# A separate opening for batch 0, and the first ternary convolution as row pairs with four products per pair

## What is computed

```python
x1  = x + deform(gn(x), w_off, b_off, w_conv)     # 3x3, offsets and masks from a 3x3 convolution with 27 outputs
q1, q2 = ternary(w1), ternary(w2)                 # -1, 0, 1 by thirds of the range of w - mean(w)
y   = gn(x1)
h1  = conv3x3(y, q1)
o1  = relu(batchnorm(h1, gamma1, beta1))          # statistics over all 4 images
o2  = batchnorm(conv3x3(o1, q2), gamma2, beta2)
out = x1 + relu(o1 + o2)
```

## Time and profile before

| | us |
|---|---|
| median of 3 executions (lowest, highest) | 3021.32 (3019.83, 3022.24) |
| the profiled execution's own time | 3026.24 |
| its span, first to last instruction | 3024.2 |
| PE busy (matmul) | 2610.6, 86% |
| DVE busy | 2101.8, 70% |
| ACT busy | 1182.2, 39% |
| POOL busy | 1354.2, 45% |
| DMA moved | 827.35 MB, 274 GB/s over the span |
| mean granted TensorE clock | 0.941 of full speed |

### The profile page before, as it was taken

How to read it: one execution, slowest core, us unless ns; L and a number is a source line. 1 busy time by engine, 2 the same in 40 slices (tenths; PEclk the granted TensorE clock), 3 DMA queues, 4 the chain that set the end, 5 groups by cost and what they waited for, 6 DMA issues and landing times. The chain is left out here.

```text
span 3024.2 us, 37569 instructions
## 1 busy us (share of the span) xinstructions
PE 2610.6 (86%) x11674; PEld 1741.7 (58%) x11674; DVE 2101.8 (70%) x4522; ACT 1182.2 (39%) x2039; POOL 1354.2 (45%) x1262
## 2 busy tenths in 40 slices
PE   3668888888999999999999998989999896999940
PEld 2444444444565555556566665555555676999940
DVE  5577778777777778777777776776766434565665
ACT  1234444444444444444444434344443112232345
POOL 1036655664554555545555555555653002333300
PEclk9879999999999999999999999999999998999975
DMA  4679999999898999989899998999997212111169
GB/s 152 176 258 347 368 355 359 344 364 318 318 339 314 338 347 349 326 307 329 315 329 334 336 315 307 329 335 324 334 329 257 94 53 67 53 56 50 51 257 408
DMA packets 277870, 827.35 MB, mean 274 GB/s; under 512 B 25436, under 2 KB 59228, under 8 KB 276964
## 3 DMA queue, kind: packets, MB, share of 16 engines
q0 software_dynamic: 165888, 604.05, 55.0%
q1 hardware_dynamic: 111844, 221.72, 21.2%
HBM read 740.19 MB, written 85.48 MB: 273 GB/s over the span
## 5 line engine op out<-in xcount | busy, mean ns | idle before, releaser
L360 POOL DMA_INDIRECT G<-pixel_pairs,quad_c x1152 | 1190.2, 1033 | 933.2 <-PE psT L785 639.0
L648 DVE SCALAR_TENSOR_TENSOR G<-G,wts_c 128x256 f32<-128x256 f32 (+1 forms) x2304 | 1259.6, 615 | 171.7 <-DMA G<-pixel_pairs,quad_c 166.9
L748 PE MATMUL psD<-ST,wconv 128*128 128x512 f32 x2304 | 1066.8, 609 | 0.0
L748 PEld LDWEIGHTS psD<-ST,wconv 128*128 128x128 f32 x2304 | 433.3, 197 | 451.0 <-issue 451.0
L410 ACT ACTIVATE G<-G,wts_c 128x256 f32<-128x256 f32 x1152 | 489.6, 497 | 419.4 <-DVE G L648 418.7
L737 PE MATMUL psF<-pf,qw 128*128 128x512 f32 x2304 | 629.4, 422 | 14.6 <-DVE pf L570 7.6
L737 PEld LDWEIGHTS psF<-pf,qw 128*128 128x128 f32 x2304 | 428.5, 189 | 163.0 <-issue 54.2
L445 ACT ACTIVATE ST<-psT 128x1024 f32<-128x1024 f32 x288 | 294.5, 1023 | 481.3 <-PE psT L785 481.1
L785 PE MATMUL psT<-idn,G 128*128 128x128 f32 x2304 | 323.8, 287 | 168.1 <-ACT G L410 167.6
L785 PEld LDWEIGHTS psT<-idn,G 128*128 128x128 f32 x2304 | 277.4, 147 | 247.0 <-issue 122.4
L737 PE MATMUL psA<-po,woff 128*64 128x512 f32 x1152 | 346.9, 449 | 6.3 <-DVE po L570 6.3
(11 more groups left out here) (144 smaller groups left out, 1604.1 us busy)
## 6 DMA issues: line engine op xcount, KB each, us to landing
pixel_pairs<-yT SPq DMA_DIRECT2D x112, 256.0 KB
G<-pixel_pairs,quad_c POOLq DMA_INDIRECT x1152, 6.4
xz<-in_x SPq DMA_DIRECT2D x32, 512.0 KB, 7.1
xres<-in_x SPq DMA_DIRECT2D x32, 512.0 KB, 7.0
x<-x1c SPq DMA_DIRECT2D x32, 512.0 KB, 4.9
h<-h1c SPq DMA_DIRECT2D x32, 512.0 KB, 3.8
out<-h SPq DMA_DIRECT2D x16, 1024.0 KB, 17.5
xo<-in_x SPq DMA_DIRECT2D x24, 640.0 KB, 7.0
```

The source lines that it names most:

```text
L360: pool.indirect_dma_start(out=G[:, i % RING, :], out_offset=None, in_=tbl[d.b].rearrange("y x q c -> (y x) (q c)"), in_offset=bass.Indirec ...
L648: dve.scalar_tensor_tensor(g[:, 0:w], g[:, w:2 * w], wts_c[:, d.p, q * NG + i:q * NG + i + 1], g[:, 0:w], ALU.mult, ALU.add).then_inc(d_ma ...
L748: ins = pe.matmul(psD[:, oc, :], wconv[:, t, k, oc * 128:(oc + 1) * 128], ST[:, k % 3, t, :], start=(k == 0 and t == 0), stop=(k == TAPS - ...
```

## The change

It has two parts.

**The opening.** Stages -2 and -1 are gone; `schedule` starts at s = 0 behind a `head()` of its own on each engine. All of x of batch 0 is loaded at once into slots 0 to 7 of the ring `G` (`x_all`), the raw w1 into the rest of the ring and `x1c`. DVE takes all statistics, ACT normalises in place, PE turns 8 x 8 blocks into `psT`, ACT evacuates into a ring of four buffers, and SP writes the whole table of batch 0. Only the first two chunks of batch 0's offset convolution are done there; chunks 2 to 7 (letter **j**) move into the first six chunks of stage 0, beside the offset convolution of batch 1. Batch 1's statistics (z) lie in the head, interleaved on DVE with the ternary form of w1; its loads are issued by SP between the table writes, each behind a wait on the statistics taken before. The statistics buffer is single from batch 2 on, and so is `xres`.

**The first ternary convolution** takes the form of the second: `planes` on DVE (four operations of 128x512), `planes_hi` on ACT, `planes_lo` on DVE, then four units of 24 matmuls of 256 columns (`f_unit`: output tile, bank), placed at taps 5, 6, 8 and 0 of the next chunk. A unit's products lie in halves of one bank; ACT copies the first (`h1_begin`), DVE adds the others (`h1_rows`: two operations of 128x256, one of 128x512, one batch-norm statistic, for each output tile). The planes `V` and the split planes `pl` are single, except in stage 4, where a second `pl_b` and `psD` are used. ACT takes over the high part of the offset convolution's split (`split_hi`). The middle weights of w1 are made in `winograd_w1`, those of w2 are copied on ACT at the end of stage 4.

```diff
-                for s in range(-2, NB + 1):
+                for s in range(0, NB + 1):
...
+                        just = (ahead(r, rh, p, 2), ahead(r, rh, p, 3)) if s == 0 else (None, None)
+                        f, before = now[3], None
+                        if f and first and s > 1:
+                            before = Chunk(s - 2, NR - 1, NR // 2 - 1, 1, False, True)
+                        elif f and not first and s < NB:
+                            before = f.before()
+                        emit(s, *now, *then, *just, before)
...
+            F_UNITS = {0: [(1, 1)], 5: [(0, 0)], 6: [(0, 1)], 8: [(1, 0)]}
+            F_UNITS_FIRST = {0: [(1, 1)], 6: [(0, 0), (0, 1)], 8: [(1, 0)]}
...
+                for r in range(NR):
+                    sp.dma_start(x_all[:, :, r * PX:(r + 1) * PX], rows_of(x, 0, r * RC, RC)).then_inc(h_load[r], 16)
...
-                    hold(sp, f_split, f.n - 1 + CREDIT)
+                    hold(sp, f_v, f.n - 1 + CREDIT)
...
+                    load_z(Chunk(1, 0, 0, 0, True, False))
+                    load_z(Chunk(1, 1, 0, 1, False, False))
...
+                    for r in range(NR):
+                        sp.wait_ge(h_yt, 2 * (r + 1))
+                        write_table(0, r, yt_ring[r % 4], h_tw[r % 4])
+                        if r == 1:
+                            sp.wait_ge(s_edge, 16 * 4 * NB)
+                            load_j(Chunk(0, 2, 1, 0, False, False))
+                        if 1 <= r < NR - 1:
+                            load_z(Chunk(1, r + 1, (r + 1) // 2, (r + 1) % 2, False, r + 1 == NR - 1))
...
                         load_z(z)
+                    if d:
+                        hold(sp, d_x1, d.n + CREDIT)
+                        sp.dma_start(xres, rows_of(x, d.b, d.r * RC, RC)).then_inc(d_xl[d.p], 16)
...
+                        write_table(o.b, o.r, yT, o_tw)
+                    for c in (fp, f if s == NB else None):
+                        if c:
+                            hold(sp, f_h, CT * (c.n + 1) + CREDIT)
+                            sp.dma_start(rows_of(h1_d, c.b, c.r * RC, RC), h1c[:]).then_inc(f_store, 16)
...
+                            pool.wait_ge(j_split, 2)
+                        else:
+                            hold(pool, o_tw, TW * (d.n + NR) + CREDIT)
+                    hold(pool, o_idx if s else j_idx, d.n + 1)
...
-                        if s == 0 and d.first and i == STAGE1:
+                        if s == 0 and d.first and i == W1_SLOT:
...
+                        y_rows(r)
+                    for r in range(NR):
+                        turned(r)
+                        if r + 3 < NR:
+                            y_rows(r + 3)
+                        if r == 4:
+                            jt_om_evac(Chunk(0, 0, 0, 0, True, False))
+                        if r == 5:
+                            jt_om_turned(Chunk(0, 0, 0, 0, True, False))
...
+                def planes_hi(s, f):
+
+                    act.wait_ge(f_v, f.n + 1 + CREDIT)
+                    act.wait_ge(f_conv, 4 * (f.n if s < NB or f.first else f.n - 1) + FC)
+                    for t in range(CT):
+                        i = act.activation(planes_of(s, f)[:, 0, t, :, 1:W + 1], V[:, t].rearrange("p j i w -> p (j i) w"), ACT.Copy)
+                    i.then_inc(f_hi, 1)
...
+                def planes(f):
+
+                    dve.wait_ge(f_y, f.n + 1)
+                    need(dve, f_hi, f.n)
+                    need(dve, f_split, f.n)
...
+                    for j, (a, b, op) in enumerate(((0, 2, ALU.subtract), (1, 2, ALU.add), (2, 1, ALU.subtract), (3, 1, ALU.subtract))):
+                        i = dve.tensor_tensor(V[:, :, j], xf[:, f.p, :, a:a + 7:2, :], xf[:, f.p, :, b:b + 7:2, :], op)
+                    i.then_inc(f_v, 1)
+
+                def planes_lo(s, f):
+
+                    dve.wait_ge(f_hi, f.n + 1)
+                    dve.wait_ge(f_v, f.n + 1 + CREDIT)
+                    p = planes_of(s, f)
+                    for t in range(CT):
+                        i = dve.tensor_tensor(p[:, 1, t, :, 1:W + 1], V[:, t].rearrange("p j i w -> p (j i) w"),
+                                              p[:, 0, t, :, 1:W + 1].bitcast(F32), ALU.subtract)
+                    i.then_inc(f_split, 1)
...
+                    dve.wait_ge(f_begin, CT * f.n + oc + 1)
+                    dve.wait_ge(f_conv, 4 * f.n + 2 * oc + 2 + FC)
...
+                    dve.tensor_tensor(odd, even, m2, ALU.subtract)
+                    dve.tensor_tensor(even, even, m2, ALU.add).then_inc(f_part, 1)
+                    dve.wait_ge(f_part, CT * f.n + oc + 1)
+                    dve.tensor_tensor(both, both, acc[:, :, 256:512].rearrange("p b (i w) -> p b i w", w=W), ALU.add).then_inc(f_h, 1)
+                    dve.wait_ge(f_h, CT * f.n + oc + 1 + CREDIT)
+                    dve.bn_stats(bn1_stats[:, oc, ds(f.n, 1), :].rearrange("p r s -> p (r s)"), h1c[:, oc, :]).then_inc(f_stat, 1)
...
+                    dve.wait_ge(h_stat, 1)
+                    norm_moments((0, 0), st0)
+                    norm_variance((0, 0))
+                    norm_scale((0, 0), scj[:], bij[:])
+                    j0, j1, j2 = Chunk(0, 0, 0, 0, True, False), Chunk(0, 1, 0, 1, False, False), Chunk(0, 2, 1, 0, False, False)
+                    dve.wait_ge(h_y, 2)
+                    jt_split(j0, x_rows(0, 9))
+                    dve.wait_ge(s_w1, 48)
+                    weight_sums(0, raw1[0][3])
+                    take_stats(Chunk(1, 0, 0, 0, True, False))
+                    weight_sums(1, raw1[1][3])
+                    step(weight_sums(2, raw1[2][3]))
+                    weight_sums_ready(3)
+                    dve.wait_ge(h_y, 3)
+                    jt_split(j1, x_rows(7, 10))
+                    take_stats(Chunk(1, 1, 0, 1, False, False))
+                    jt_indices(j0, 0)
+                    jt_indices(j0, 1)
+                    weight_extremes(0)
+                    weight_limits(0)
+                    compare_w1(0)
+                    take_stats(Chunk(1, 2, 1, 0, False, False))
+                    take_stats(Chunk(1, 3, 1, 1, False, False))
+                    compare_w1(1)
...
+                    winograd_w1()
+                    jt_split(j2, xf_rows(j2))
+                    jt_indices(j1, 0)
+                    jt_indices(j1, 1)
+                    for r in range(4, NR):
+                        take_stats(Chunk(1, r, r // 2, r % 2, False, r == NR - 1))
+                    dve.wait_ge(z_stat, 2 * NR + CREDIT)
+                    norm_moments((0, 1), st0)
+                    norm_variance((0, 1))
+                    norm_scale((0, 1), sc0[:], bi0[:])
+                    split_lo(Chunk(1, 0, 0, 0, True, False))
...
+                        if f and d and k == f_planes_step(f):
+                            planes(f)
+                        if fp and k == (2 if d else 0):
+                            h1_rows(s - 1 if f.first else s, fp, 1)
+                        if f and d and k == f_planes_step(f) + 2:
+                            planes_lo(s, f)
...
+                        if f2 and not d and k == 2:
+                            planes(f2)
+                            planes_lo(s, f2)
...
+                    acc, p = acc_of(s, oc), planes_of(s, f)
+                    if bank == 0:
+                        if oc == 0:
+                            if s == 1 and f.first:
+                                pe.wait_ge(s_tern, 1)
+                            pe.wait_ge(f_split, f.n + 1)
+                        pe.wait_ge(f_h, CT * f.n + CREDIT + (oc if s < NB else 0 if oc or f.first else -1))
+                    for half, j in enumerate(((1, 0), (2, 3))[bank]):
+                        for dx in range(3):
+                            for t in range(CT):
+                                w = wino[:, t, dx] if j == 2 else qw[:, t, (0, 3, None, 6)[j] + dx]
+                                for part in range(2):
+                                    ins = pe.matmul(acc[:, bank, half * 256:half * 256 + 256].rearrange("p (h w) -> p h w", w=W),
+                                                    w[:, oc * 128:(oc + 1) * 128], p[:, part, t, 4 * j:4 * j + 4, dx:dx + W],
+                                                    start=(dx == 0 and t == 0 and part == 0),
+                                                    stop=(dx == 2 and t == CT - 1 and part == 1))
+                    ins.then_inc(f_conv, 1)
...
+                    group_sums((0, 0))
+                    pe.wait_ge(s_woff, 1)
+                    for r in range(3):
+                        turn(r)
+                    for tap in range(4):
+                        jt_conv(j0, tap)
+                    turn(3)
+                    for tap in range(4, TAPS):
+                        jt_conv(j0, tap)
+                    turn(4)
+                    turn_extremes(0)
+                    turn(5)
+                    jt_turn_om(j0)
+                    for tap in range(4):
```

(10 more changed lines are left out.)

475 lines of the change are left out of this document (332 added, 143 removed).

## The result

The changed kernel takes 2933.9 us in the median of 4 runs (2929.3 to 2936.2), the kernel before 3021.8 us beside it; the ratio is 0.9704, with an interval of 0.969 to 0.9719. That is 88 us less. The forecast was 131 less, 2890 us.

What follows compares the result with a forecast made beforehand. It took the DMA queues to bound stage 0, PE stages 1, 2, 4 and the second block, and a handshake bubble stage 3. Terms -80 + 13 - 68 + 4 = -131 against the median of 3021.3 gave 2890 us, range 2840 to 2960.

Steps and rivals of the forecast that it cites:

- Opening, -80: Before DVE's first combining operation: one DVE chain summing to 82 us, so that operation comes at 117 to 118, not 198.
- Stage 0, +13: Deformable convolution of batch 0: six chunks get a j chunk and take 64.5 us against 62.3; ends 0 and +30.
- Stages 1 to 3, -68: Eight chunks each: 68.4 to 66.3, 68.4 to 64.9 and 63.0 to 60.1 us, giving -17, -28 and -23.
- With PE at 60 the DMA queues decide: Stages 1 to 3: with PE's work down from 67.0, the queues need 65.6, 64.2 and 59.4 us a chunk.
- 355.5 GB/s: DMA rate of the old stage 0, 22.15 MB in 62.3 us a chunk, taken as the queues' ceiling.
- Stage 3's bubble goes: Stage 3: DVE's 7.3 us wait a chunk at h1's statistics vanishes, as it no longer waits behind the last tap.
- Stage 4, +4: Last stage, conv1 alone: SP's order keeps a chain of 18.7 us a chunk, before 18.8; ends -45 and +20.
- Rival 2: Last stage becomes PE-bound if the load is let go earlier: chunks at 12 to 13 us, 2841 us; chance 0.12.
- Rival 1: Ring stalls on DVE's order, conv1 gives nothing in stages 1 to 3, stage 0 goes to 65: 2967 us; chance 0.18.
- Rival 5: DVE bounds the chunk: pitches 71.9, 70.5 and 65.7 in stages 1, 2 and 3, slower at 3040 us; chance 0.03.
- The marks: Profile signs set beforehand: first combining time, chunk pitches, DMA share, PE busy and clock, no h1 wait, stage 4 at 18 to 19 us.

Runs made afterwards that it cites:

- e5: Changed kernel without the loads of x for the residual (0.52 MB a chunk) from batch 1 on; 2931.2 us.
- e6: Changed kernel with each gathered row half as long (2 KB in place of 4 KB) from batch 1 on; 2907.4 us.
- e7: Changed kernel with four more unused DVE operations (2.8 us) in each chunk of batches 1 to 3; 2964.3 us.
- e9: Kernel before the change, with every gathered row but those of the first chunk half as long; 3005.6 us.
- e8: Changed kernel with conv1's third quarter moved from tap 8 to tap 0 of the next chunk, the fourth from tap 0 to 1; 2930.5 us.
- e3: Changed kernel; in the last stage SP issues the load of conv1's next rows before waiting for and storing the previous chunk's h1; 2908.1 us.
- e1: Changed kernel with batch 0's offset convolution moved from taps 0-3 to taps 1-5, its index chain wholly at tap 8; 2910.4 us.

## Why the prediction was right, and where it was not

The direction and the range of 2840 to 2960 held; the forecast was 44 us too low, and the time lies outside the forecast's own range of 2865 to 2920. That the range held is luck in part: batch 0 missed by 58 us, and the rest gave 17 of them back, most of it in stages whose limit had been read wrongly. Step by step:

- **Opening, -80.** Right: the first combining operation came at 119.5, forecast for 117 to 118, and it was the chain on DVE that I had summed, with two waits for batch 1's rows at its end. Those waits were smaller than I charged (7.9 us, not 14), and 14 us of others filled the place, of which the sum had at most a part; the longest is 4.6 for ACT's first rows of batch 1. In this the total is luck.
- **Stage 0, +13, with ends at 0 and +30.** This is the step that failed: "PE rises to about 64 at the lower clock and 60 at full clock; DVE to 56. With 22.81 MB the DMA limit is 64.2 us. I take 64.5." Measured +71.5: +20.8 in the first chunk (84.6 us for 63.8), +56.5 in the next five (73.8 us each), -5.9 in the last two. The step took the chunk as the largest of its engines' sums. The runs show that the parts add up in time instead: four heavy taps on PE, two of them 8.3 us, then a piece of 9.2 us on DVE, between engines that can be apart by three taps only. PE's 62.6 us of work and the 11.2 that it waits for combined and scaled rows (56.0 over five chunks) make up the 73.8. I had also counted six j chunks, but none of them as the first of the program, where nothing runs ahead. That the added work was summed correctly (PE 63.5, DVE 55.7) made the number look safe.
- **Stages 1 to 3, -68.** Measured -83: -30.4, -33.2 and -19.4, in pitches 65.4, about 64 and 61.3, forecast 66.3, 64.9 and 60.1. The numbers are close and **the reason was wrong**, so this part came out by luck. "With PE at 60 the DMA queues decide" does not hold: e5 takes bytes away and nothing follows, e6 takes more than 40% of them and 1.1, 1.5 and 0.3 us a chunk follow. In stages 1 and 2 PE is nearly full (61.7 of 65.4 at clock 1.00), but DVE is on the path as well (e7: 1.9 and 1.0 us a chunk of 2.8); no run took work from PE there. Stage 3 is PE and DVE in turn. What I had taken as a price, 355.5 GB/s, is about what the loop of that kernel happened to ask for: without 43% of its bytes it is only 2.6 us a chunk faster (e9). A term was too small besides: the 96 products of conv1 take 13.6 us in the chunk of batch 1 (72 of them 9.9, the other 24 3.7), 0.142 each, where 0.123 gave 11.8, so PE is busy 61.7 and not 60.
- "Stage 3's bubble goes." Its place did: no wait at the statistics of h1. But DVE stands 7.4 us at PE's last tap instead, since a quarter of conv1 at tap 8 lies ahead of it. e8 takes 2.3 us from this wait and 2.6 from the chunk.
- **Stage 4, +4.** Right in its mechanism, shown by e3, and in its size: 18.9 us a chunk for 18.7 forecast, and +0.3 together with the second block (+1.7 up to its first product, -1.3 behind it). Rival 2, the last stage bound by PE, was told apart by SP's order, rightly; e3 is that rival made true, worth 26 and not 49.
- **Rival 1** (the ring stalls on DVE's order) had 0.18 and was put in the wrong stages: it was judged for 1 to 3 and decided stage 0. Its argument against, "the ring holds three taps, 20 us", counts only where nothing else already uses the ring up. In stages 1 to 3 DVE's order costs something too, as e7 shows, but it doesn't take conv1's gain away. Rival 5, the same place priced higher, did not come; its own pitches add up to 3024 us, not to the 3040 that it names.
- **The marks** set out for the profile: first operation at 115 to 125, yes; batch 0 at 64 to 65, no; 66, 65 and 60 after it, nearly; share at 0.96 or more, PE below 93% and clock below 1.00 in stages 1 and 2, no (0.95, 94% and 1.00 in the window above), and these were the hint that the queues were not what ended the chunks there; stage 4 below 70% PE with ACT waiting for xf, yes (108.65 of 160).

## What to carry to other kernels

When work is added to a loop of several engines, sum it by piece and place, not by engine alone: ask in which taps each engine has no slack, and how long the longest piece is that it does between two steps for its neighbour, against the depth of the ring between them. Here 2.5 us taken out of a piece of 9 came back almost whole, and three moves that take no instruction away gave 64 us in all. A share of 0.95 on a queue, like 90% on an engine, doesn't show a limit; halving the transfers does, and it needs one line.

## What the runs showed of the hardware that was not expected

The queues' share and their GB/s don't go together by one number. In the 10.5 us behind its first combining operation the changed kernel moved more than in any steady chunk, nearly all of it gathers with rows of 4 KB; and with rows of half the size (e9 above) 210 GB/s already took a share of 0.69: by that 304 GB/s for a full share, an estimate, against 371 (360 / 0.97) with rows of 4 KB. Windows of the changed kernel:

```profile
119.50:130.00 10.50, 2.49 (x10) 2.21 (x11) 7.16 (x14) 2.22 (x5) 6.19 (x6) 0.50 1.03 409
```

So the price of 355.5 GB/s in the prediction was not a ceiling even for this traffic: in e1 a whole chunk of batch 0 (545.06 to 605.26) moved 367 GB/s, at a share of 0.99. Whether 409 can be held for a whole chunk no run here shows.
